# Hardware loops over the head pairs, and score banks in rotation, in a fused attention and feed-forward kernel

## Reference

```python
q, k, v, g = n @ Wq.T, n @ Wk.T, n @ Wv.T, n @ Wg.T     # 16 heads of 128; rope on q and k
s = clip(n @ Ws1.T @ Ws2.T + bs2, -32, 32)              # 64 slots per head
z = cumlogsumexp(s, time); es = exp(s); enz = exp(-z)
A = tril(q @ k.T) * scale
qv = softmax(enz * (A @ es))                            # over the 64 slots
W2 = tril((qv * enz) @ es.T)
o = W2 @ v
attn = (rms_norm(o) * g_norm * silu(g)) @ Wo.T
ffn = (gelu(n @ Wgate.T) * (n @ Wup.T)) @ Wdown.T       # 4-bit weights with scales
```

## Time and profile before

| | |
|---|---|
| median of 3 runs | 1156.71 us (1156.29 to 1158.56) |
| the profiled execution | 1156.29 us, span 1154.6 us |
| PE busy | 1108.5 us, 96% |
| DVE busy | 948.3 us, 82% |
| ACT busy | 640.3 us, 55% |
| POOL busy | 421.8 us, 37% |
| DMA | 23.03 MB, 20 GB/s on average |

### The profile page before, as it was taken

One profiled execution on the slowest core, in us unless ns is written; L12 is line 12 of the kernel. 1 busy time (PEld: TensorE's weight loads), 2 busy tenths in 40 slices (PEclk: granted clock), 3 DMA queues, 4 the chain that ended last, 5 costly groups with the idle time before them and its releaser, 6 DMA issues.

```text
span 1154.6 us, 19869 instructions
## 1 busy us (share of the span) xinstructions
PE 1108.5 (96%) x6872; PEld 936.6 (81%) x6872; DVE 948.3 (82%) x1808; ACT 640.3 (55%) x1748; POOL 421.8 (37%) x306
## 2 busy tenths in 40 slices
PE   5779999999999999999999999999999999999995
PEld 4568888888888888888888888888888888888884
DVE  5978888788888889889887888878888888888863
ACT  4455466555645556555655555565564555655551
POOL 4323244422424335232453324443252434523131
PEclk9899999999999999999999999999999999999998
DMA  4002000020002000020000100001000200000001
GB/s 161 1 1 75 2 1 1 1 76 1 2 1 76 1 1 2 1 76 1 1 1 1 75 1 1 2 18 58 1 1 2 75 2 1 2 1 19 9 12 37
DMA packets 9108, 23.03 MB, mean 20 GB/s; under 512 B 816, under 2 KB 5808, under 8 KB 7984
## 3 DMA queue, kind: packets, MB, share of 16 engines
q1 hardware_dynamic: 9008, 21.76, 5.2%
HBM read 19.66 MB, written 2.10 MB: 19 GB/s over the span
## 4 chain that ended last, share of the span: by engine, by line
PE 82%; DVE 5%; issue 4%; ACT 2%; POOL 1%; POOLq 0%; DVEq 0%; ACTq 0%
PE bank L194 19%; PE bank L196 18%; PE bank L195 18%; PE bank L283 4%; PE bank L315 3%; PE bank L340 3%; PE bank L296 3%; PE bank L329 2%; PE bank L285 2%; PE bank L331 2%; PE bank L332 2%; DVE og L759 1%; PE bank L299 1%; PE bank L307 1%; PE bank L273 1%
## 5 line engine op out<-in xcount | busy, mean ns | idle before, releaser
L1085 POOL TENSOR_TENSOR inter_lo<-ffb,inter_hi 128x512 fp32r<-128x512 f32 x64 | 83.3, 1326 | 425.1 <-ACT inter_hi L607 425.1
L1076 POOL TENSOR_TENSOR qkT<-ra,xs 128x512 f32<-128x512 f32 x128 | 164.4, 1285 | 109.5 <-DVE xs L850 77.4
L576 ACT ACTIVATE sm<-bank,mx 128x64 f32<-128x64 f32 x256 | 76.4, 324 | 122.0 <-DVE mx L806 122.0
L847 DVE TENSOR_TENSOR ra<-bank,rope 128x512 f32<-128x512 f32 x128 | 87.7, 685 | 53.1 <-ACT xs L558 51.9
L795 DVE RECIPROCAL enzT<-enzT 128x256 f32<-128x256 f32 x64 | 111.5, 1742 | 0.0
L850 DVE TENSOR_TENSOR xs<-xs,rope 128x512 f32<-128x512 f32 x128 | 110.6, 864 | 0.0
L194 PE MATMUL bank<-xh,wqk_hi 128*128 128x512 f32 x256 | 110.4, 431 | 0.0
L194 PE MATMUL bank<-xh,wgu_hi 128*128 128x512 f32 x256 | 106.1, 414 | 0.5 <-POOL wgu_lo L1055 0.5
L581 ACT ACTIVATE At<-bank 128x128 f32<-128x128 f32 x128 | 35.4, 276 | 126.7 <-DVE At L730 126.6
L194 PE MATMUL bank<-wvg_hi,xh 128*128 128x512 f32 x256 | 103.8, 405 | 0.0
L196 PE MATMUL bank<-xh,wgu_lo 128*128 128x512 f32 x256 | 102.1, 399 | 0.0
(11 more groups left out here) (137 smaller groups left out, 3202.4 us busy)
## 6 DMA issues: line engine op xcount, KB each, us to landing
raw<-in_w_qkvg SPq DMA_DIRECT2D x8, 1024.0 KB, 5.1
scaled<-in_w_scaled SPq DMA_DIRECT2D x8, 640.0 KB, 7.6
packed<-in_w_packed SPq DMA_DIRECT2D x8, 384.0 KB, 5.7
acc<-in_x SPq DMA_DIRECT2D x4, 512.0 KB, 7.6
out<-acc SPq DMA_DIRECT2D x4, 512.0 KB, 2.9
ws_raw<-in_w_slot SPq DMA_DIRECT2D x8, 48.0 KB, 1.7
rope<-in_rope_tab SPq DMA_DIRECT2D x1, 256.0 KB, 5.8
osq<-in_w_slot SPq DMA_DIRECT2D x1, 128.0 KB, 3.9
```

The source lines that it names most:

```text
L576: ins = act.activation(sm[:, c], src[:, c], ACT.Exp, bias=mx[:, g:g + 1], accum_out=ssum[:, g:g + 1])
L847: dve.tensor_tensor(two(ra[i % 2][:, :]), two(pj[i][:, :]), cos, ALU.mult).then_inc(cos_done, 1)
L1076: pool.tensor_tensor(qkT[:, i, :], ra[i % 2][:, :], xs[i % 2][:, :], ALU.add).then_inc(roped, 1)
L1085: pool.tensor_tensor(inter[1][e][:, :], ffb[e][:, :], inter[0][e][:, :].bitcast(F32), ALU.subtract).then_inc(inter_lo, 1)
```

## The change

Two things are changed together. First, `each_stage` writes out the four stages of hp = 0 and of hp = 7, and runs hp = 1 to 6 as a loop on each engine (`eng.Fori(1, HP - 1)`) whose body is four stages; SP's loop over the weight loads becomes a loop of 7 turns too. In the loops `hp` is a register, and every wait value and every DMA address that contains it is worked out from that register. Second, the uses of the two `sc` banks get numbers, eleven in a stage, and alternate between the banks (`sc_bank`); E becomes the eleventh use and leaves `rg[1]`. With it go changes of order: on PE `project_vg` 2 comes ahead of `slot_rows`, `project_qk` 3 ahead of `slot_weights` 1, and E between `values` 0 and `values` 1; on ACT `swap_halves` 3 comes ahead of `off_diagonal` 2 and 3, and `copy_J` goes from ahead of `off_diagonal` 0 to between the two `square_o`; on DVE `rope_cos` 2 and `rope_sin` 2 come ahead of `diagonal` 2 and 3.

```diff
+SC_SLOTS = {"A": (0, 1, 2, 3), "S": (4,), "K": (5,), "W": (6, 7, 8, 9), "E": (10,)}
+SC_STEP = 11
...
+        def sc_bank(bp, kind, i=0):
+            return sc[(SC_STEP * bp + SC_SLOTS[kind][i]) % 2]
...
         def each_stage(eng, stage):
 
-            for hp in range(HP):
+            for bp in range(BP):
+                stage(0, bp, bp == 0, False)
+            with eng.Fori(1, HP - 1) as hp:
                 for bp in range(BP):
-                    stage(hp, bp, hp == bp == 0, hp == HP - 1 and bp == BP - 1)
+                    stage(hp, bp, False, False)
+            for bp in range(BP):
+                stage(HP - 1, bp, False, bp == BP - 1)
...
-            for hp in range(HP - 1):
+            with sp.Fori(0, HP - 1) as hp:
...
                 for i in (0, 1):
-                    if first:
-                        pe.wait_ge(clip_done if i == 1 else J_ready, 1)
+                    if first and i == 1:
+                        pe.wait_ge(clip_done, 1)
+                    elif first or i == 1:
+                        pe.wait_ge(J_ready, st + 1)
                     else:
-                        pe.wait_ge(W_off, 4 * st - 1 + i)
+                        pe.wait_ge(W_off, 4 * st)
                     scores(st, bp, i, hp)
...
                 if not first:
                     outputs(st, 0, php, None)
-                elif not last:
+                if not last:
                     project_vg(st + 1, nbp, nhp, 2, True)
-                slot_rows(st)
-                if not first and not last:
-                    project_vg(st + 1, nbp, nhp, 2, True)
+                slot_rows(st, bp)
...
                 pe.wait_ge(qe_ready, st + 1)
-                if not last:
-                    pe.wait_ge(es_ready, st + 2)
-                    slot_transpose(rg[1], esT[nbp % 2])
+                pe.wait_ge(A_off, 4 * st + 4)
+                if not last:
                     pe.wait_ge(clip_done, st + 2)
                 slot_weights(st, bp, 0)
                 if not last:
                     project_qk(st + 1, nbp, nhp, 2)
...
+                if not last:
+                    project_qk(st + 1, nbp, nhp, 3)
                 pe.wait_ge(W_off, 4 * st + 2)
                 slot_weights(st, bp, 1)
-                if not last:
-                    project_qk(st + 1, nbp, nhp, 3)
...
                 values(st, bp, 0)
+                if not last:
+                    pe.wait_ge(es_ready, st + 2)
+                    pe.wait_ge(W_off, 4 * st + 3)
+                    slot_transpose(sc_bank(bp, "E", 0), esT[nbp % 2])
...
                     swap_halves(st + 1, 1)
-                    copy_J(st + 1, rg[1][:, :])
                 off_diagonal(*w_args, 0, 1.0)
                 off_diagonal(*w_args, 1, 1.0)
...
                     swap_halves(st + 1, 2)
+                    swap_halves(st + 1, 3)
                 off_diagonal(*w_args, 2, 1.0)
                 off_diagonal(*w_args, 3, 1.0)
-                if not last:
-                    swap_halves(st + 1, 3)
...
                 square_o(st, 0)
+                if not last:
+                    copy_J(st + 1, sc_bank(bp, "E", 0)[:, :])
                 square_o(st, 1)
...
+                if not last:
+                    rope_cos(st + 1, 2)
+                    rope_sin(st + 1, 2)
                 diagonal(*w_args, 2, mask_w, (o_full, 2 * st))
                 diagonal(*w_args, 3, mask_w, (o_full, 2 * st))
                 if not last:
-                    rope_cos(st + 1, 2)
-                    rope_sin(st + 1, 2)
                     rope_cos(st + 1, 3)
```

More of the change, by code:

```diff
@@ L267, in slot_scores @@
                     pe.wait_ge(ws2_lo, 4 * hp + 4)
-                pe.matmul(sc[0][:, :] if n is not None else sc[1][:, :],
+                pe.matmul(sc_bank((bp - 1) % BP, "S")[:, :] if n is not None else sc[1][:, :],
                           ws2[:, :], h1[:, bp, :], start=True, stop=True).then_inc(S_full, 1)
@@ L280, in scores @@
                     pe.wait_ge(roped, 4 * st + 2 * h + 2)
-                dst = sc[b]
+                dst = sc_bank(bp, "A", i)
                 t0 = b * T
@@ L300, in slot_reads, with slot_rows @@
                 mm.then_inc(ok_full, 1)
-            def slot_rows(st):
+            def slot_rows(st, bp):
                 pe.wait_ge(okz_done, st + 1)
-                dst = sc[1]
+                dst = sc_bank(bp, "K")
                 for i in range(NT):
@@ L312, in slot_weights @@
                 t0 = b * T
-                pair = [(sc[h], slice(h * M, (h + 1) * M)) for h in range(2)]
+                pair = [(sc_bank(bp, "W", 2 * b + h), slice(h * M, (h + 1) * M)) for h in range(2)]
                 for dst, g in pair:
@@ L378, in transpose_x @@
                     if bp == 3 and k == 1:
-                        pe.wait_ge(J_ready, 2)
+                        pe.wait_ge(qe_ready, 1)
                     for i in range(NT):
@@ L493, in stage @@
                     pe.wait_ge(h1_lo, 4)
-                elif not last:
-                    pe.wait_ge(J_ready, st + 2)
                 values(st, bp, 1)
@@ L567, in copy_J, with softmax_exp @@
                 act.activation(esJ[:, :, :].rearrange("p n m -> p (n m)"), src, ACT.Copy).then_inc(J_ready, 1)
-            def softmax_exp(st):
+            def softmax_exp(st, bp):
                 act.wait_ge(mx_done, st + 1)
@@ L572, in softmax_exp @@
                 wait(act, rs_done, st)
-                src = sc[1]
+                src = sc_bank(bp, "K")
                 for g in range(8):
@@ L577, in softmax_exp, with off_diagonal @@
                 ins.then_inc(p_ready, 1)
-            def off_diagonal(diag, done, dst, st, i, scale):
+            def off_diagonal(diag, done, dst, bp, kind, st, i, scale):
                 act.wait_ge(diag, 4 * st + i + 1)
-                act.activation(dst[i][:, 1, :], sc[i % 2][:, P:2 * P], ACT.Copy,
+                act.activation(dst[i][:, 1, :], sc_bank(bp, kind, i)[:, P:2 * P], ACT.Copy,
                                scale=scale).then_inc(done, 1)
@@ L652, in stage @@
                 npar = (bp + 1) % 2
-                a_args = (A_diag, A_off, At, st)
-                w_args = (W_diag, W_off, Wt, st)
-                more = hp < HP - 1
+                a_args = (A_diag, A_off, At, bp, "A", st)
+                w_args = (W_diag, W_off, Wt, bp, "W", st)
+                more = not (isinstance(hp, int) and hp == HP - 1)
                 off_diagonal(*a_args, 0, SCALE)
@@ L683, in stage @@
                     prepare_out(hp + 1)
-                softmax_exp(st)
+                softmax_exp(st, bp)
                 if not last:
@@ L699, in stage @@
                     split_slot(hp + 1)
+                if first:
+                    x_hi(3)
                 if not last:
                     swap_halves(st + 1, 2)
-                if first:
-                    x_hi(3)
+                    swap_halves(st + 1, 3)
                 off_diagonal(*w_args, 2, 1.0)
                 off_diagonal(*w_args, 3, 1.0)
-                if not last:
-                    swap_halves(st + 1, 3)
                 if first:
@@ L724, in two, with diagonal @@
                 return ap.rearrange("p (b t) -> p b t", b=2)
-            def diagonal(full, done, dst, st, i, mask, used):
+            def diagonal(full, done, dst, bp, kind, st, i, mask, used):
                 dve.wait_ge(full, 4 * st + i + 1)
                 wait(dve, *used)
-                src = sc[i % 2][:, 0:3 * P].rearrange("p (n t) -> p n t", n=3)
+                src = sc_bank(bp, kind, i)[:, 0:3 * P].rearrange("p (n t) -> p n t", n=3)
                 dve.tensor_tensor(dst[i][:, 0:3:2, :], src[:, 0:3:2, :], mask[:, :, :], ALU.mult).then_inc(done, 1)
@@ L801, in softmax_in, with softmax_max @@
                 dve.tensor_tensor(okz[:, :], rg[0][:, :], enzT[par][:, :], ALU.mult).then_inc(okz_done, 1)
-            def softmax_max(st):
+            def softmax_max(st, bp):
                 dve.wait_ge(K_full, st + 1)
                 wait(dve, p_ready, st)
-                dve.tensor_reduce(mx[:, :], sc[1][:, :].rearrange("p (g m) -> p g m", m=M),
+                dve.tensor_reduce(mx[:, :], sc_bank(bp, "K")[:, :].rearrange("p (g m) -> p g m", m=M),
                                   AX_X, ALU.max, negate=True).then_inc(mx_done, 1)
@@ L936, in stage @@
                 par, npar, pbp = bp % 2, (bp + 1) % 2, (bp - 1) % BP
-                more = hp < HP - 1
-                a_args = (A_full, A_diag, At, st)
-                w_args = (W_full, W_diag, Wt, st)
+                more = not (isinstance(hp, int) and hp == HP - 1)
+                a_args = (A_full, A_diag, At, bp, "A", st)
+                w_args = (W_full, W_diag, Wt, bp, "W", st)
                 if bp == 3 and more:
@@ L967, in stage @@
                 if not last:
-                    clip(st + 1, npar, sc[0][:, :])
+                    clip(st + 1, npar, sc_bank(bp, "S")[:, :])
                 if not first:
@@ L983, in stage @@
```

(2 more changed lines are left out.)

## The result

| | before | after |
|---|---|---|
| median | 1156.65 us (1156.29 to 1158.56) | 1187.7 us (1184.56 to 1188.98) |
| ratio, 95% interval | | 1.0261 [1.0238, 1.0284] |
| the profiled execution | 1156.29 us, span 1154.6 | 1186.13 us, span 1184.4 |

What follows compares the result with a forecast made beforehand. PE was taken to bound the kernel, with next to no waiting to win back. 1156.3 - 4.7 + 7.8 - 3.0 + 10.0 + 2.4 gave 1168.8, say 1169 us; range 1161 to 1176, 8 in 10 within 1149 to 1190.

Steps and rivals of the forecast that it cites:

- What bounds the kernel: PE, busy 1108.5 of 1154.6 us, has about 4 us of waiting to win back; new losses add to the time.
- The stream: On PE, one float32/fp32r alternation fewer per stage: 0.15 us for 31 stages, -4.7 us (bounds -9.3 and 0).
- The wait at E: On PE, transposes E wait for `off_diagonal` 2: +0.25 us for 31 stages, +7.8 us (bounds 0 and 18.6).
- rival C: At the loop's jumps back, a bare fetch plus slow clock: 23.5 us for five jumps, 1182 us; chance 0.17.
- Line 340's wait: At `gated_transpose` on PE, an earlier `square_o` 1 removes 3.0 of 3.7 us of waiting (bounds -3.7 and 0).
- The jumps: At the loop's five jumps back, fetches partly covered by queued matmuls: 2.0 us each, +10 us (bounds 0 and 27).
- Register values: In the 24 loop stages, uncovered waits on values from registers: 0.1 us a stage, +2.4 us (bounds 0 and 11).
- Rival D: In 24 loop stages, register values pace a chain, 0.46 us each, E's wait 18.6 us: 1191 us; chance 0.10.
- SP's loads: On SP, weight-load addresses from a register cost nothing, covered by stages 0 and 1 of a head pair.

Runs made afterwards that it cites:

- order-only kernel: The changed kernel with everything written out, no loops, only banks and order changed: 1180.44 us, 1.0196 against the kernel before.
- the shortened split: Against the order-only kernel, POOL's split of `wgu` works on 8 of 512 columns from the second head pair on: 1158.95 us, 0.9999 of the kernel before.
- e3_dve_back: The order-only kernel with DVE's diagonals 2 and 3 back ahead of rope 2: 1169.21 us, 1.0089 against the kernel before.

## Why the prediction went wrong, by its own steps

**What bounds the kernel** was right: PE had no slack, and what it lost anew was added to the time.

**The stream** (-4.7). Nothing came of it: the stages without a wait of their own take 33.8 to 34.0 us in the kernel before and 34.0 in the order-only kernel. Whether the alternation that went was worth its 0.15 us, and something else took it back, no run singles out.

**The wait at E** (+7.8, bounds 0 to 18.6): this is the step that failed. It had the right instructions and the wrong duration. In ordinary stages it held: 0.19 to 0.42 us in the kernel after, where I took 0.25. But "cosine and sine, 0.6 us apart each" came from one stage and was multiplied by 31. In the seven stages with bp = 3 that have a split of `wgu` the sine takes 2.45 to 2.47 us beside it, `diagonal` 2 is late by 1.8 us more, and PE idles 2.1 us. The row was in the trace of before, at 593.24, in a place where it cost nothing. The group of all 128 sines would have shown it too: mean 864 ns against the 0.68 us of most. The price is shown by the shortened split, 21.5 us. Between the two profiled executions the difference is 14.7 us: the seven stages with bp = 3 are 13.4 us shorter (35.9 to 36.6 against 34.1 to 34.3 us), and two stretches at the lower clock behind such a wait are gone. The order-only kernel's four times run from 1174.39, the profiled one, to 1184.33. What the others lost on top is in no trace, but the mean granted clock of each is on record: 0.985 and 0.983 in the two shorter ones, 0.976 in the two longer. By that, an estimate (0.024 of 1182 us lost against 0.015 of 1173, at half the clock), the longer ones ran some 21 us more at 1.2 GHz, in which a busy PE loses half, about 10 us: the difference that was measured, 9 to 10. So the wait at E has a second price that the prediction gave only to rival C's jumps.

**Line 340's wait** (-3.0) went as said; that it is `osq`'s one buffer that holds it is shown by the second buffer. Without POOL's stretch the order is worth 0.9999, against my +0.1 us. That the sum came out is in part luck: the stream gave nothing in place of -4.7, and E waits 4.8 us there in place of 7.8.

**The jumps** (+10): by the ratios 7.2 us (0.0062 of 1158) between the loops with and without the hint, and 8.0 between the kernel after and its hinted form. The gaps in the kernel after are 2.0 to 2.5 us at four of the five places and 0.8 at one, against my 2.0. At that one PE's queued matmuls ran at the lower clock, 0.21 us apart in place of 0.11, and so covered more of the 3.67 us that the jump took. The term's mechanism held, a fetch in part covered by queued matmuls; "a fetch of 2.7" was too short, and so was the cover, half of 1.34 us. That the other engines' fetches would lie beside PE's did not matter: their jumps show none (0.06 us or less). Rival C had a part: in the kernel after PE runs 3.4 us at a granted clock of 0.50, 1.2 GHz, behind two of the jumps (611.2, 894.5), and the stage then takes 35.79 in place of 34.16 us, 1.6 us, where I had worked out 1.5. It does so behind two of the waits at E as well (184.5, 324.5). The row of one:

```profile
611.20:614.60 3.40, 3.40 (x11) 2.81 (x10) 1.69 (x5) 0.55 (x2) 0.96 (x1) 0.50 0.00 0
```

The 128 KB on TensorE that the Trainium skill gives in Advanced Engine Details and Errata, "ISA Cache", agree with the hinted loop: seven blocks of 16.4 KB, 115 KB, stay on chip. The "Only 2 cache lines!" of the same section does not. Without the hint the body was fetched again each turn although it would have fitted, and the measurement decides. My estimate of 108 ns for a jump compares with 45 to 63 ns on DVE, ACT and POOL, 216 to 257 ns on PE with the hint and 3.3 to 3.8 us without.

**Register values** (+2.4): at most 0.6 us in the old order, 1 to 2 us in the new one, read from the lengths of the stages. Rival D falls: jumps and clock apart, no stage in the loop is longer by more than 0.2 us than the same stage of the written-out kernel of its order. **SP's loads**: nothing, as said.

**Not foreseen**: the 2.4 us won in the head. The sum in measured terms is 22.7 (order, 0.0196 of 1158) + 8.0 (jumps) - 2.4 (head) = 28.3 of the 30.2 us that the ratio gives; register values in the new order are a part of the 1.9 us left, and the intervals of the parts are wider than that. The profiled execution gives the same picture: waits at E 20.2, jumps 9.7, lower clock 6.2, less 3.7 at line 340 and 2.3 in the head, are 30.1 of the 29.8 us by which the span grew.

The sign was right, but I got most of it from the jumps, and the order is the larger part. The time measured lies inside my wide range and 6 us from rival C's 1182; that is luck, since C gave 23.5 us to the jumps and nothing more than I did to the order. The largest term stood in a step that I had costed from one stage.

## What to carry to other kernels

Before moving an instruction ahead of one that PE waits for, read every execution of it in the trace, not one: its longest duration, in the stage where it is longest, is what the move puts on the path. Here the mean stood a quarter over the usual duration (864 against 681 ns), and that was the sign. Look there for what POOL does at the same moment. And the loops here, in the old order, cost next to nothing with the back edge hinted, and some 1.5 us a jump without.

## What the runs showed of the hardware that was not expected

- A DVE instruction of 0.68 us took 2.37 to 2.47 us beside a GpSimd one of 2.35 us, and 1.43 us beside one of 1.27 us (`e3_dve_back`), and ended 0.55 us after it in both cases; the GpSimd one took no longer than its like elsewhere.
- An unhinted jump back lasted 3.3 to 3.8 us on PE and 0.04 to 0.06 us on DVE, ACT and POOL. Unhinted, PE fetched its loop body of seven blocks anew every turn (66 blocks in all); hinted, it kept it (21 blocks), the jump lasted 0.22 to 0.26 us, and the gap was gone.
- Waits on register values cost at most 0.1 us in 136 us of work in the old order, 0.2 to 0.3 us in the new one.
- A wait of 2 us, of PE on another engine or at a jump, was followed in some cases (4 of 12 in the kernel after) by a stretch at 1.2 GHz, which cost 1.6 us more.
